# Normalised linear attention on 16 images: new places in the order for the last keys chunk, the maxima, the loads and the evictions

## The reference

```python
x: (16, 64, 64, 256)                      # 16 images of 4096 positions, 256 channels
h = group_norm(x, groups=32, eps=1e-5)    # mean and variance over an image and 8 channels
q, k, v = split(h @ W_qkv)                # (4096, 256) each
k = softmax(k over the 4096 positions)
context = k^T v                           # 256 x 256, one matrix per image
out = x + (q @ context) @ W_out + b_out
```

## Time and profile before

| | us |
|---|---|
| median of 3 runs (lowest, highest) | 1199.64 (1195.49, 1200.19) |
| the profiled execution, its own time | 1202.58 |
| its span, first to last instruction | 1200.6 |
| PE busy | 1166.4 (97% of the span) |
| DVE, ACT, POOL busy | 931.0, 836.3, 627.0 (78%, 70%, 52%) |
| DMA | 266.70 MB, mean 222 GB/s |
| mean granted TensorE clock | 0.998 |

### The profile page before, as it was taken

The page is one execution under the profiler, slowest core; times in us unless marked ns, Lnnn a source line. Parts: engine busy times, 40 slices in busy tenths (PEclk is TensorE's granted clock), DMA queues, the critical chain, the costliest instruction groups (busy, mean ns, idle before and its releaser), DMA issues.

```text
span 1200.6 us, 21468 instructions
## 1 busy us (share of the span) xinstructions
PE 1166.4 (97%) x8206; PEld 1089.3 (91%) x8206; DVE 931.0 (78%) x2008; ACT 836.3 (70%) x1146; POOL 627.0 (52%) x305
## 2 busy tenths in 40 slices
PE   4999999999999999999999999999999999999998
PEld 3889999989899898998989999899999989999996
DVE  6988779787796877878787797878869788796561
ACT  5667768677685776857777676776857768577764
POOL 7655563645656355553655636456463655536530
PEclk9999999999999999999999999999999999999999
DMA  8438666586766758657486665867657586573524
GB/s 318 163 134 315 228 216 236 179 296 214 258 212 202 263 188 280 228 201 250 165 316 228 215 232 179 303 212 261 214 199 271 179 295 227 198 254 119 190 84 162
DMA packets 107078, 266.70 MB, mean 222 GB/s; under 512 B 10208, under 2 KB 10208, under 8 KB 106976
## 3 DMA queue, kind: packets, MB, share of 16 engines
q1 hardware_dynamic: 106976, 265.33, 63.7%
HBM read 198.18 MB, written 67.11 MB: 221 GB/s over the span
## 4 chain that ended last, share of the span: by engine, by line
PE 82%; DMA 6%; DVE 4%; ACT 3%; issue 2%; POOL 1%; SPq 1%; DVEq 0%; ACTq 0%; POOLq 0%
PE ps_k L460 24%; PE ps_e L625 18%; PE ps_e L634 9%; PE ps_e L542 5%; PE ps_e L554 5%; PE ps_e L544 5%; DMA xs<-in_xt_dram 4%; PE ps_g L554 4%; PE ps_g L544 4%; PE ps_g L542 4%; PE ps_g L573 1%; PE ps_g L590 1%; DMA x_raw<-in_xn_dram 1%; DVE bn L922 1%; DVE e_raw L1054 1%
## 5 line engine op out<-in xcount | busy, mean ns | idle before, releaser
L387 POOL TENSOR_TENSOR xt_lo<-xt_raw,xt_hi 128x1024 fp32r<-128x1024 f32 x128 | 307.5, 2404 | 458.8 <-ACT xt_hi L738 194.1
L393 POOL TENSOR_TENSOR x_lo<-x_raw,x_hi 128x1024 fp32r<-128x1024 f32 x128 | 282.4, 2225 | 59.9 <-ACT x_hi L743 50.5
L994 DVE TENSOR_TENSOR mx<-ps_k,mx 128x256 f32<-128x256 f32 x480 | 203.1, 423 | 72.0 <-ACT e_raw L747 50.2
L795 ACT ACTIVATE o_stage<-ps_e,bias 128x512 f32<-128x512 f32 x253 | 168.8, 687 | 105.5 <-PE ps_e L634 101.5
L460 PE MATMUL ps_k<-wk_hi,xt_hi 128*128 128x256 f32 x1024 | 205.9, 283 | 1.4 <-DVE mx L994 1.2
L460 PE MATMUL ps_k<-wk_lo,xt_hi 128*128 128x256 f32 x1024 | 205.0, 282 | 0.0
L747 ACT ACTIVATE e_raw<-ps_k 128x512 f32<-128x512 f32 x256 | 141.2, 595 | 78.1 <-PE ps_k L460 78.1
L755 ACT ACTIVATE e_hi<-e_raw 128x1024 fp32r<-128x1024 f32 x128 | 134.8, 1053 | 67.2 <-DVE e_raw L1054 45.4
L922 DVE BATCH_NORM_STATS2 bn<-xs 128x6 f32<-128x512 f32 x240 | 153.8, 685 | 33.2 <-DMA xs<-in_xt_dram 31.9
L460 PEld LDWEIGHTS ps_k<-wk_hi,xt_hi 128*128 128x128 f32 x1024 | 164.3, 189 | 10.6 <-issue 2.4
L460 PE MATMUL ps_k<-wk_hi,xt_lo 128*128 128x256 f32 x1024 | 157.5, 282 | 0.0
(11 more groups left out here) (147 smaller groups left out, 2027.6 us busy)
## 6 DMA issues: line engine op xcount, KB each, us to landing
xt_raw<-in_xt_dram SPq DMA_DIRECT2D x128, 512.0 KB, 4.6
x_raw<-in_xn_dram SPq DMA_DIRECT2D x128, 512.0 KB, 3.8
out_dram<-o_stage SPq DMA_DIRECT2D x127, 512.0 KB, 4.5
xs<-in_xt_dram SPq DMA_DIRECT2D x240, 256.0 KB, 5.0
w_setup<-in_w_dram SPq DMA_DIRECT2D x2, 256.0 KB, 9.7
out_dram<-o_stage SPq DMA_DIRECT2D x2, 256.0 KB, 2.0
wk<-in_w_dram SPq DMA_DIRECT2D x1, 256.0 KB, 10.0
wq_t<-in_w_dram SPq DMA_DIRECT2D x1, 256.0 KB, 11.0
```

The source lines that it names most:

```text
L387: nc.gpsimd.tensor_tensor(xt_lo[:, s], xt_raw[:, s], xt_hi[:, s].bitcast(F32), ALU.subtract).then_inc(xt_lo_ready, 1)
L393: nc.gpsimd.tensor_tensor(x_lo[:, s], x_raw[:, s], x_hi[:, s, :, 0:C].bitcast(F32), ALU.subtract).then_inc(x_lo_ready, 1)
L795: nc.scalar.activation(o_stage[:, u % O_SLOTS, h, :], src, ACT.Identity, bias=bias[:, h:h + 1]).then_inc(o_ready, 1)
L994: nc.vector.tensor_tensor(mx[:], tile, mx[:], ALU.max).then_inc(max_done, 1)
```

## The change

No instruction is added or taken away, apart from one subtraction to `e_lo` (chunk 2 of image 0) that goes from POOL to DVE. What changes is the order.

- PE: keys 7 come directly behind keys 6 (ahead of emit 6), and emit 6 and 7 follow in a row. In the gather `spread_max(b, 1)` stands before `gather_low(b, 0)`.
- DVE: two more half chunks of statistics before `key_maxes(n, 3)` and fewer behind `block_diag(n, 0)`; the second maximum (`block_max(n, 1)` to `block_scales`) ahead of `e_low(n, 2)` instead of at the start of the gather.
- ACT: emit 4 ahead of the exponentials of chunk 0; `xt_high(7)` ahead of the exponentials of chunk 1; the exponentials of chunk 2 around emit 6; `xt_high(2)` behind the gather.
- SP: the `xs` loads ahead of the store, at other emitted chunks; the last `xt` load of a period (chunk 2) goes between the `x` loads of the next gather.
- Image 0: all of these orders anew.

```diff
-XS_AFTER = {0: (4, 8), 2: (8, 12), 3: (12, 16)}
-FIRST_XT = (8, 11, 15)
-POOL_LOW = 3
+XS_AHEAD = {0: (4, 8), 1: (8, 12), 2: (12, 14), 4: (14, 16)}
+FIRST_XT = (11, 13, 15)
+FIRST_X = (6, 7, 8, 9)
+POOL_LOW = 2
...
             for q in range(S_SLOTS, CB * NCH):
-                if q < 2 * X_SLOTS:
-                    load_x(0, q - X_SLOTS)
                 sp.wait_ge(bn_done, NCH * CB + q - S_SLOTS + 1)
                 load_xs(1, q)
+                if q in FIRST_X:
+                    load_x(0, FIRST_X.index(q))
...
                     load_x(b, j)
+                    if more and b and j == X_SLOTS + 1:
+                        sp.wait_ge(e_ps, b * (CB * NCH))
+                        load_xt(n, 1 - parity, EMIT_ORDER[NCH - 1])
...
                 for u, j in enumerate(EMIT_ORDER):
-                    if more2 or (more and j not in DOUBLED):
+                    if u < NCH - 1 and (more2 or (more and j not in DOUBLED)):
                         sp.wait_ge(e_ps, b * (CB * NCH) + CB * u + CB)
...
+                    if more2 and u in XS_AHEAD:
+                        for q in range(*XS_AHEAD[u]):
+                            sp.wait_ge(bn_done, b * (NCH * CB) + 2 * NCH * CB + q - S_SLOTS + 1)
+                            load_xs(b + 2, q)
                     if b == B - 1 and u == NCH - 1:
                         store_last()
                     elif not late(b, u, CB - 1):
                         store(b, u)
-                    if more2 and u in XS_AFTER:
...
# POOL
-                if more and b:
+                if b == 0:
+                    pool.wait_ge(e_lo_ready, e_lo_count(0, HALF - 1))
+                elif more:
                     pool.wait_ge(var_parts_ready, n)
...
# PE
+                def first_gather():
+                    gather(0, 0)
+                    gather_high(0, 1)
+                    gather_high(0, 2)
+                    gather_low(0, 1)
+                    spread_max(0, 1)
+                    gather_high(0, 3)
+                    gather_low(0, 2)
+                    gather_low(0, 3)
+                    gather(0, 4)
+                    stats_mean(1)
+                    gather(0, 5)
+                    gather_high(0, 6)
+                    stats_var(1)
+                    gather_low(0, 6)
+                    gather(0, 7)
+                def gather_steps():
+                    gather_high(b, 0)
+                    if more:
+                        stats_mean(n)
+                    spread_max(b, 1)
+                    gather_low(b, 0)
+                    gather_high(b, 1)
+                    if more:
+                        stats_var(n)
+                    gather_low(b, 1)
+                    for j in range(2, NCH):
+                        gather(b, j)
...
                     if more:
-                        if u < NCH - 1:
+                        if u < NCH - 2:
                             keys(n, np_, u + 1)
+                        if u == NCH - 3:
+                            keys(n, np_, NCH - 1)
...
# ACT, image 0 and the emitting part
             for j in range(X_SLOTS):
-                x_high(0, j)
                 keys_out(0, j, 0)
                 keys_out(0, j, 1)
+                x_high(0, j)
...
                 both_out(4)
+                emit(b, 4)
                 if more:
                     exps(n, 0)
-                emit(b, 4)
                 if more:
                     xt_high(n, np_, 6)
                 both_out(5)
                 if more:
+                    xt_high(n, np_, 7)
                     exps(n, 1)
                 emit(b, 5)
-                if more:
-                    xt_high(n, np_, 7)
                 both_out(6)
+                both_out(7)
+                if more:
+                    exp_high(n, 2)
                 emit(b, 6)
                 if more:
-                    exps(n, 2)
-                both_out(7)
+                    exp_exact(n, 2)
                 emit(b, 7)
...
# DVE, image 0
-            for q in range(1, 5):
+            for q in range(1, 7):
                 bn_half(1, q)
             for j in range(HALF):
                 key_maxes(0, j)
-                for q in ((5, 6), (7, 8), (9,), ())[j]:
+                for q in ((7, 8), (9, 10), (11,), ())[j]:
                     bn_half(1, q)
...
# DVE, period
                 key_maxes(n, 2)
-                bn_halves(4, 8)
+                bn_halves(4, 10)
                 key_maxes(n, 3)
                 block_max(n, 0)
                 block_diag(n, 0)
-                bn_halves(8, 12)
+                bn_halves(10, 11)
                 shift(n, 0)
                 key_maxes(n, 4)
+                bn_halves(11, 12)
                 shift(n, 1)
...
                 key_maxes(n, 7)
+                block_max(n, 1)
+                block_diag(n, 1)
+                block_scales(n)
                 e_low(n, 2)
```

113 lines of the change are left out of this document (56 added, 57 removed).

## The result

The changed kernel takes **1211.60 us** (median of 4 executions, 1208.69 to 1211.98); the kernel before took 1197.82 us beside it (1195.49 to 1200.19). The ratio is 1.0112, 95% interval [1.0089, 1.0134]: **1.1% slower**, where 0.7% faster was forecast. The profiled execution took 1208.69 us, with a span of 1206.6.

The account below looks back on a forecast made before the run. PE was taken as the bound, busy 1166.4 of 1200.6 us, with only waits recoverable: -8.2 (middle) - 2.0 (image 0) + 0.3 (last image) = -9.9 from 1202.58 gives 1192.7, adjusted to 1191.2 us; range 1186.5 to 1199.0.

Parts of the forecast that it names:

- Statistics and `xs` loads: Middle periods: half chunk 9 lands near 173.6 with loads taking 4.7 to 5.2 us; key_maxes(3) up to 0.6 us late.
- the 0.88 us of slack: First diagonal of a middle period: finished at 178.03, asked for by PE at 178.91, so 0.6 us of delay fits.
- rival B: Middle periods: half chunks 8 and 9 come too late, PE waits 1.8 us in each of 14, 1213.4 us; chance 0.08.
- The sum's starting point: Whole kernel: sum starts from the profiled 1202.58 us, then half its 2.94 us above the median is taken off.
- Emit 4: ACT, ahead of chunk 0's exponentials: PE's 1.55 us stall goes; exponentials 0.6 us later, covered by 1.3 us.
- Keys 7 behind keys 6: PE, middle periods: slacks of 0.38 and 0.2 us, cost taken at 0.2 us a period, 3 us in 14.
- Stores 1 to 2 us later: Middle periods: each store goes 1 to 2 us later, covered by two staging buffers and a chunk of keys.
- `xt` of chunk 2: Load into the gather, conversion behind it: the 2.5 us of waits for x_lo go, with cover on ACT.
- Image 0: First image, new orders: -2.0 us taken, bounds -4.4 and +2.0; keys 2 about 1 us late, keys 6 about 1.5.
- the port was freed "for certain": Image 0: moving e_lo of chunk 2 to DVE frees 1.28 us by the port rule, term nearer -3.
- Rival C: Image 0: the clock falls again, 1.75 us stay and are paid perhaps twice, 1193 to 1194.7 us; chance 0.12.
- Last image: Second spread_max of the last image: 1.25 us waited instead of 0.97, a term of +0.3 us.

Follow-up runs that it names:

- e8: Changed kernel without loading half chunks 8 to 11 of images 2 to 15, their statistics taken from half chunks 4 to 7: 1196.07 us, ratio 0.9986.
- e17: e14, with GpSimd starting the last xt_lo of a period (chunk 7) after VectorE's e_lo of chunk 1: 1194.21 us, ratio 0.9972.
- e4: Kernel before with one edit, the evictions of emit 4 ahead of the exponentials of chunk 0: 1200.02 us, ratio 1.0017.
- e14: e13, with emit 4 also ahead of the exponentials of chunk 0 on ScalarE: 1199.18 us, ratio 1.0010.
- e13: Kernel before with the edits of e12, and GpSimd in image 0 starting x_lo of chunk 5 after mean_parts is written: 1195.49 us, ratio 0.9975.
- e1: Changed kernel, with the middle periods' VectorE statistics and xs loads as before, loads behind the store again: 1200.14 us, ratio 1.0014.
- e11: Changed kernel, statistics ordered as before, half chunks 4 to 11 loaded ahead of the stores, 12 to 15 at the fourth emitted chunk: 1202.85 us, ratio 1.0035.
- e12: Kernel before, with the xt load of chunk 2 among the gather's x loads and its conversion behind the gather: 1196.09 us, ratio 0.9983.
- e16: Changed kernel, image 0 with half chunks 1 to 4 ahead of the first maxima and the later statistics spread: 1207.07 us, ratio 1.0072.

## Why the prediction was wrong

Taken by its steps.

- **Statistics and `xs` loads: the step that failed.** The issue time was right (18.0 us into the period against 17.9). What failed was "with two fewer 512 KB transfers ahead I take 4.7 to 5.2". The load of half chunk 8 took 5.8 us, the median of the four 5.1 and the shortest 4.5. Half chunk 9 left 0.3 us later than forecast and took 5.6 us, so the maxima of chunk 3 began 1.6 us later in the period than before instead of 0.6, and the 0.88 us of slack didn't hold. By `e8` this step cost the middle periods 12.2 us, nearly what the waits at `u_hi` come to (11.7 us on the weight side). Without it the rest of the middle came as forecast: 1010.0 us, where the sum has 1019.1 - 8.2 = 1010.9. The range taken was a guess about the queue; nothing in the earlier trace rows (5.6 at the least) supported a value under 5.6. It counted two transfers of 512 KB less ahead, and left out that half chunks 4 to 7 were now right ahead: in the 4.9 us before the load of half chunk 8 SyncE issued 2 MB, as in the undisturbed period of before. That this kept the time long fits, but no run isolates it. By the text's own rival B, 5.8 us is past the point where it decides (5.2).
- **Rival B had the mechanism and the wrong point.** It put 6.1 us as the latency from which the kernel is slower, on the assumption that all 11.2 us of waits go at the same time. At 5.8 us PE waited 0.58 us in the period shown, and 8.9 us in 14 periods by the table of waits (11.7 on the weight side), not the 1.8 each of a latency of 7.0. Measured by `e8`, the step took away more than the whole middle was to give (12.2 against 8.2 us). That B's 1213.4 us lies near the measured median is chance in part: its middle was +14 us and came as +3.1, its image 0 was -2.0 and came as +2.6, and the median of the changed kernel is 2.9 us above its profiled execution.
- **The sum's starting point.** The profiled execution of 1202.58 us was an unusually long one: in the batches of the study the median of before was 1197.6 to 1198.6. I wrote that such differences are themselves waits of the kind that go, and then took off half of 2.94 us. But the sum had already taken all 11.2 us of that execution's middle waits away, so 1.5 us of them went twice. It is the gain that is smaller: against a typical execution of before, 1192.7 is 5 to 6 us, and of the 11.2 us in the middle only some 7 were there (an estimate: 11.2 less the 4 to 5 us by which the profiled execution was slow). `e17`, whose profiled middle is at the floor but for 0.7 us, got 3.3 us by the medians (1197.55 against 1194.21), and 6.2 in its fastest execution, the profiled one of 1191.36.
- **Emit 4.** The stall went as forecast (7.1 to 0.9 us). The cover I named, "1.3 against 0.6 us", looked at VectorE and ScalarE only. The 0.6 us moved `e_lo` 1 onto GpSimd's `xt_lo` 7, and on the kernel before the step was worth nothing (`e4`) or less (`e14`) until a wait took the race away (`e17`). Even with the wait no gain of emit 4 itself is shown: `e17` and `e13` have ratios of 0.9972 and 0.9975 to the kernel before beside them.
- **Keys 7 behind keys 6**: taken at 3 us in 14 periods, measured at 2.1 or less together with the whole rest (`e8`), and at 2.7 us in 4 waits with the statistics in their old places (`e1`). About right. The second `spread_max` waits in one middle period of `e8`, by 0.2 us on the weight side.
- **Stores 1 to 2 us later, covered by two buffers.** ScalarE's evictions waited 74.1 us in sum, PE for them 0.9 in the changed kernel and 3.4 in `e11`. Right in the main.
- **`xt` of chunk 2**: the middle periods' gain is real (`e12` beats before), but "costs nothing" was wrong in the old order of image 0, by 2 us of PE's wait at `mean_parts`.
- **Image 0: -2.0 forecast, +2.6 measured.** The delay of the keys was taken at 1 us (keys 2) and 1.5 us (keys 6) and came as 2.02 and 1.91 us at keys 2 and 3; before, PE's waits at the keys were 0.98 and 0.21 us, so this is 2.7 us more. Behind them the clock fell as well, which the next point counts at 1.7 us. These two make 4.4 us, and the other moves gave 1.8 of them back. `e16`, with two statistics less ahead of the first maxima, starts image 1 4.0 us sooner. In the gather the subtraction of the earlier trace rows went down to 0.15 us as forecast, and its neighbour `mean_parts` took 1.14 us in its place. That the port was freed "for certain" was true of one instruction and not of the list.
- **Rival C came true beside B**, in its words "paid perhaps twice": the granted clock fell in image 0 at two places. From 68 to 76 us its means were 0.72 and 0.85, which is 4 x 0.28 + 4 x 0.15 = 1.7 us at the full rate, as much as before. From 32 to 40 us they were 0.95 and 0.62, which is 4 x 0.05 + 4 x 0.38 = 1.7 us more, and before there was no such fall there.
- **Last image**: +0.3 forecast. From its first keys to the end of the span it took 1206.6 - 1102.96 = 103.6 us, before 1200.6 - 1097.23 = 103.4. Right.

Put together, against the span of before: image 0 +2.6, the middle +3.1, the last image +0.3, in sum the 6.0 us between the two spans; the rest of the 13.8 us between the medians is that the profiled execution of before was a slow one and that of the changed kernel its fastest. The sign was set by a value for one transfer, which the rows at hand had contradicted.

## What to carry to other kernels

A duration that is read from rows behind a deeper queue may be taken shorter only as far as some row shows it; where a step lives on the difference, the forecast belongs to the row and the hope to the rival. Where a fixed order is nearly full, a move is to be checked against the lists of all engines, and above all against the pair that shares a resource: here VectorE and GpSimd, when both subtract from two operands in SBUF. A difference of 0.03 us in who starts first was worth 2.2 us, and a wait on the engine that has time (GpSimd, 52% busy) made `e14` both faster and steadier (`e17`). And the profile of one execution is to be set against the median of many before its waits are counted as a gain.

## What the runs showed of the hardware

**VectorE and GpSimd exclude each other for whole instructions where both subtract operands in SBUF.** VectorE's `e_lo<-e_raw,e_hi`, both operands in SBUF, took 1.22 us alone and up to 3.46 behind GpSimd's `xt_lo` of 2.41; the other way round `xt_lo` took 3.21 us. Even a subtraction of 2 elements a partition waits that long (0.16 to 2.14 us). The same subtraction with one operand in PSUM was never held up in `e14`, though GpSimd worked beside it there as well (64 of them, min/median/max):

```profile
L1065 DVE TENSOR_TENSOR e_lo<-ps_k,e_hi x64: 1211/1224/1226, 63.5 to 1160.6; 128x1024 fp32r<-128x1024 f32 x64
```

The Trainium skill (SBUF — State Buffer, "SBUF: two separate sides") states just this: the shared port pair goes to whichever instruction starts first, for its whole length, and VectorE needs it for an operation with two SBUF inputs. The traces agree in every case looked at. That a collision can set the time of a kernel whose two engines are busy for 78% and 52% of the span was not to be expected from their shares.

**Four loads put ahead of a store did not arrive sooner.** Half chunks 4 to 7 went out ahead of the store, from 166.50 on (13.1 us into the period), and took 3.3 to 5.6 us, 5.0 in the median. Before, they stood behind the store, went out from 13.4 us into the period on and took 4.4 to 4.9 us, 4.6 in the median. From 169 to 173 us, while they and the store were under way, the transfers moved less than later (columns as above; the last two are the DMA share and GB/s):

```profile
169.00:171.00 2.00, 2.00 (x10) 1.63 (x9) 1.72 (x4) 0.69 (x1) 2.00 (x2) 1.00 0.88 244
171.00:173.00 2.00, 2.00 (x10) 1.59 (x10) 0.69 (x1) 1.64 (x2) 1.01 (x2) 1.00 0.80 261
173.00:175.00 2.00, 2.00 (x16) 1.87 (x15) 1.32 (x2) 0.00 (x0) 2.00 (x1) 1.00 1.04 389
```

244 to 261 GB/s at a share of 0.80 to 0.88, against 389 at 1.04. The engines were near their full share in all three. Why they moved less is open: the loads of 256 KB bring 2 KB to each partition and those of 512 KB bring 4 KB, but no experiment changed only that.
